# Tile numbers packed four to a word, and an alternating order of adds in the joint pass of a graph network kernel

## The reference

```
x = layernorm(x + gated(x))      # a_in  = segment_sum(f_in[src] * w,  dst); a_out = segment_sum(f_out[dst] * w2, src)
x = layernorm(x + relational(x)) # agg   = segment_sum((x @ W[type])[src], dst)
x = layernorm(x + attention(x))  # softmax over the edges of a node, segment_max and segment_sum
x = layernorm(x + relational(x)) # agg   = segment_sum((x @ W[type])[dst], src)
```

## Time and profile before

| | |
|---|---|
| time, median of 3 runs | 8551.53 us (8549.6 to 8559.96) |
| span of the profiled execution | 8619.9 us |
| busy: PE, DVE, ACT, POOL | 4852.2, 3573.0, 1730.7, 5243.4 us |
| granted TensorE clock, mean | 0.742 |

### The profile page before, as it was taken

How to read it: one execution, slowest core, us unless ns; L and a number is a source line. 1 busy time by engine, 2 the same in 40 slices (tenths; PEclk the granted TensorE clock), 3 DMA queues, 4 the chain that set the end, 5 groups by cost and what they waited for, 6 DMA issues and landing times. The chain is left out here.

```text
span 8619.9 us, 69117 instructions
## 1 busy us (share of the span) xinstructions
PE 4852.2 (56%) x17004; PEld 2990.1 (35%) x17004; DVE 3573.0 (41%) x9196; ACT 1730.7 (20%) x7055; POOL 5243.4 (61%) x5610
## 2 busy tenths in 40 slices
PE   3202235555557777777455543777777876655554
PEld 1100014444435555543333332222223663333332
DVE  4201014333335555564222224444445776244445
ACT  0000001111123333322000002222223874000000
POOL 5577756666666666632666662666665882366665
PEclk6655557777778888888666666878888998866666
DMA  3001012222235555554333335656666884333333
GB/s 96 2 3 39 15 40 90 90 89 89 91 116 176 177 175 175 177 114 156 92 93 93 92 93 67 186 184 187 187 187 177 267 271 156 117 93 92 91 94 85
DMA packets 422550, 1037.69 MB, mean 120 GB/s; under 512 B 159993, under 2 KB 188189, under 8 KB 415516
## 3 DMA queue, kind: packets, MB, share of 16 engines
q0 software_dynamic: 223616, 552.46, 22.9%
q1 hardware_dynamic: 198556, 480.95, 17.4%
HBM read 716.74 MB, written 316.30 MB: 120 GB/s over the span
## 5 line engine op out<-in xcount | busy, mean ns | idle before, releaser
L944 POOL DMA_INDIRECT rel_rows<-relation_rows,rel_ring_row x1640 | 1558.3, 950 | 1177.7 <-ACT rel_ring_end L937 695.1
L956 PE MATMUL rel_sums<-rel_rows,rel_hot 128*128 128x256 f32 x3280 | 1197.1, 509 | 1178.3 <-issue 448.5
L956 PEld LDWEIGHTS rel_sums<-rel_rows,rel_hot 128*128 128x128 f32 x3280 | 785.7, 252 | 1590.1 <-issue 1076.9
L982 DVE TENSOR_TENSOR g_acc<-rel_sums,g_acc 128x256 f32 x1224 | 517.8, 423 | 1532.9 <-DMA records_by_dst<-g_big 548.5
L1913 POOL DMA_INDIRECT nmax_rows<-messages,nmax_ring_row x832 | 788.6, 948 | 566.3 <-ACT nmax_ring_row L1869 327.6
L761 POOL DMA_INDIRECT rows_by_src<-spread_rows,spread_ring_place x832 | 803.2, 965 | 483.8 <-issue 254.3
L838 POOL DMA_INDIRECT both_rows<-batch_normed,both_ring_row x832 | 791.0, 951 | 460.9 <-ACT both_ring_end L807 231.3
L605 POOL DMA_INDIRECT records_by_dst<-sort_ring_rec,sort_ring_place x784 | 810.4, 1034 | 390.6 <-issue 241.2
L739 PE MATMUL spread_p_r<-g_big,spread_hot_t 128*128 x1664 | 631.5, 545 | 542.0 <-ACT spread_hot_t L674 358.8
L1961 DVE TENSOR_TENSOR g_big<-nmax_short,g_big 128x512 f32 x832 | 575.7, 692 | 659.9 <-PE nmax_short L1934 288.6
L1934 PE MATMUL nmax_short<-nmax_rows,g_ident_b 128*128 128x512 bf16 x2496 | 800.3, 436 | 0.0
(11 more groups left out here) (443 smaller groups left out, 6114.8 us busy)
## 6 DMA issues: line engine op xcount, KB each, us to landing
kept_rows<-nmax_rows SPq DMA_DIRECT2D x208, 536.0 KB
g_big<-kept_rows SPq DMA_DIRECT2D x208, 536.0 KB
both_out_rows<-rows_by_src SPq DMA_DIRECT2D x202, 520.0 KB
att_local_row<-local_of_edge SPq DMA_DIRECT2D x52, 512.0 KB
rel_rows<-relation_rows,rel_ring_row POOLq DMA_INDIRECT x1640
relation_rows<-mix_table SPq DMA_DIRECT2D x25, 1024.0 KB
relation_rows<-fin_table SPq DMA_DIRECT2D x25, 1024.0 KB, 3.9
rows_by_src<-spread_rows,spread_ring_place POOLq DMA_INDIRECT x832
```

Of the source, the lines that this page charges most:

```text
L944: pool.indirect_dma_start(rows[:, j, 0:words], None, table, bass.IndirectOffsetOnAxis(ap=ring_row[:, j:j + 1], axis=0)).then_inc(landed[n ...
L956: last = nc.tensor.matmul(sums[:, unit % slots, 0:width], hot[:, j, :], rows[:, j, :], start=of == 0, stop=of == GRAIN[k] - 1)
L982: nc.vector.tensor_tensor(at, sums[:, unit % slots, 0:width], at, ALU.add).then_inc(added, 1)
```

## The change

The tile numbers are packed. `sort_edges` keeps `unit_tile` as a tile of its own and, when the last places are worked out, folds four numbers, of 5 bits each, into one 32-bit word of `g.unit_word[k]`: three small instructions on DVE for each list, with a wait behind each. `tiles_of` loads 4 words in place of 16 numbers and returns 16 expressions (shift by 5n, mask with 31). At each place that uses a tile number, `compute_val` works out shift and mask into a register of that engine; for the adds this stands ahead of the wait for the add before.

In the joint pass the order of DVE changes. Before, one step was four out adds, four matrices, two in adds of the same group. Now step n is out add, in add, out add, in add, out add, two matrices, out add, two matrices, and its in adds belong to group n-1.

```diff
+            for k in range(2):
+                word, tile = g.unit_word[k][0:1, :], unit_tile[k][0:1, 0:PACK * WORDS[k]]
+                for n in reversed(range(PACK - 1)):
+                    c.step(nc.vector.scalar_tensor_tensor(word, tile[:, PACK - 1::PACK] if n == PACK - 2 else word,
+                                                          float(B32), tile[:, n::PACK], ALU.mult, ALU.add))
+                    c.wait()
...
             def target(k, acc, unit):
                 if unit % 16 == 0:
                     tiles[k][:] = tiles_of(nc, mybir.EngineType.DVE, g, k, unit)
-                return acc[:, bass.ds(tiles[k][unit % 16], 1), 0:width].rearrange("p t d -> p (t d)")
+                tile = nc.vector.compute_val(tiles[k][unit % 16])
+                return acc[:, bass.ds(tile, 1), 0:width].rearrange("p t d -> p (t d)")
...
-            build(0)
-            build(1)
-            for n in range(GROUPS):
-                if n < OUT_GROUPS:
-                    add_out(n)
+            def step(n):
+                outs = list(range(n * PER[1], (n + 1) * PER[1])) if n < OUT_GROUPS else []
+                ins = list(range((n - 1) * PER[0], n * PER[0])) if n else []
+                if outs:
+                    dve.wait_ge(out_summed, n + 1)
+                    add_out(outs[0])
+                if ins:
+                    dve.wait_ge(summed, n)
+                for at in range(PER[0]):
+                    if ins:
+                        add_in(ins[at])
+                    if outs:
+                        add_out(outs[at + 1])
                 if n + 2 < GROUPS:
-                    build(n + 2)
-                add_in(n)
+                    build(n + 2, 0, GRP // 2)
+                if outs:
+                    add_out(outs[-1])
+                if n + 2 < GROUPS:
+                    build(n + 2, GRP // 2, GRP)
...
 def tiles_of(nc, engine, g, k, unit):
 
-    return nc.values_load_multi_w_load_instructions(
-        g.unit_tile[k][0:1, unit:min(unit + 16, CHUNKS[k] // GRAIN[k])], engines=[engine], min_val=0, max_val=T,
-        skip_runtime_bounds_check_because="sort_edges counts them up from 0 and cuts them off at T")[1]
+    first = unit // PACK
+    words = nc.values_load_multi_w_load_instructions(
+        g.unit_word[k][0:1, first:min(first + 16 // PACK, WORDS[k])], engines=[engine], min_val=0,
+        max_val=T * sum(B32 ** n for n in range(PACK)),
+        skip_runtime_bounds_check_because="each packs PACK numbers that sort_edges cuts off at T")[1]
+    return [nc.s_assert_within((word >> (5 * n)) & (B32 - 1), 0, T,
+                               skip_runtime_bounds_check_because="sort_edges cuts every number off at T")
+            for word in words for n in range(PACK)]
```

More of the change, by code:

```diff
@@ L47 @@
 GROUPS = CH // GRP
+PACK = 4
+WORDS = tuple(chunks // grain // PACK for chunks, grain in zip(CHUNKS, GRAIN))
 CHP = -(-(P * EC + BUCKETS * (2 * P - 1)) // (2 * P)) * 2 + GRP
@@ L220, in sort_edges @@
         ones_last = m.sb("ones_last", [P, P])
+        unit_tile = [m.sb(f"unit_tile_{k}", [P, CHP // GRAIN[k]], I32) for k in range(2)]
         p_mean = m.ps("p_mean", [P, 2, 512])
@@ L866, in _, with build @@
             tiles = [[], []]
-            def build(n):
+            def build(n, lo, hi):
                 dve.wait_ge(staged, n + 1)
-                for j in range(slot(n).start, slot(n).stop):
+                for j in range(slot(n).start + lo, slot(n).start + hi):
                     last = nc.vector.tensor_scalar(hot[:, j, :], g.iota[:, 0:P], ring_end[:, j, 0:1],
                                                    ring_end[:, j, 1:2], ALU.is_equal, ALU.mult)
-                last.then_inc(hot_ready, 1)
+                if hi == GRP:
+                    last.then_inc(hot_ready, 1)
             def target(k, acc, unit):
@@ L877, in target @@
                     tiles[k][:] = tiles_of(nc, mybir.EngineType.DVE, g, k, unit)
-                return acc[:, bass.ds(tiles[k][unit % 16], 1), 0:width].rearrange("p t d -> p (t d)")
[L880 to L894, removed]
-            build(0)
-            build(1)
-            for n in range(GROUPS):
-                if n < OUT_GROUPS:
-                    add_out(n)
-                if n + 2 < GROUPS:
-                    build(n + 2)
-                add_in(n)
+                tile = nc.vector.compute_val(tiles[k][unit % 16])
@@ new lines, in target, with add_out, add_in @@
+                return acc[:, bass.ds(tile, 1), 0:width].rearrange("p t d -> p (t d)")
+            def add_out(unit):
+                at = target(1, g.acc2, unit)
+                if unit:
+                    dve.wait_ge(out_added, unit)
+                nc.vector.tensor_tensor(at, out_sums[:, unit % 4, 0:width], at, ALU.add).then_inc(out_added, 1)
+            def add_in(unit):
+                at = target(0, g.acc[:], unit)
+                if unit:
+                    dve.wait_ge(added, unit)
+                nc.vector.tensor_tensor(at, sums[:, unit % 4, 0:width], at, ALU.add).then_inc(added, 1)
@@ L904, in _ @@
+            for n in range(2):
+                build(n, 0, GRP)
+            for n in range(GROUPS + 1):
+                step(n)
             dve.wait_ge(added, GROUPS * PER[0])
@@ L1956, in _ @@
                     tiles = tiles_of(nc, mybir.EngineType.DVE, g, 0, unit)
+                if c % GRAIN[0] == 0:
+                    tile = nc.vector.compute_val(tiles[unit % 16])
                 dve.wait_ge(scored, c + 1)
@@ L2527, in build @@
         g.rec = [m.sb("rec_0", [P, CHP, RW]), m.sb("rec_1", [P, CHP, 2])]
-        g.unit_tile = [m.sb(f"unit_tile_{k}", [P, CHP // GRAIN[k]], I32) for k in range(2)]
+        g.unit_word = [m.sb(f"unit_word_{k}", [P, WORDS[k]], I32) for k in range(2)]
         make_constants(nc, g)
```

18 lines of the change are left out of this document (12 added, 6 removed).

## The result

The changed kernel takes 8571.14 us (median of 19 runs), the kernel before 8555.24 us beside it: ratio 1.0018, 95% interval [1.0012, 1.0024]. That is 16 us more, just inside the 0.2% that counts as no change here, and sure to be no gain. Forecast were 8496 us and a range of 8390 to 8570; the time lies outside it. One of the 19 runs took 8899 us at a granted clock of 0.59; the ratio goes by the others. A later set of runs gave 1.0018 [1.0009, 1.0027] again.

The account below looks back on a forecast made before the run. The prediction took POOL's indirect DMAs as the bound, with DVE counting only where POOL waits. Gains of 77 us (joint pass 50) less 22 us added gave -55 us: 8551.5 to 8496 us, range 8390 to 8570.

Parts of the forecast that it names:

- The bound: Joint pass: POOL's indirect DMAs and short gaps set a floor of 1049 us; about 203 us more is waiting for ACT.
- The sign that the prediction named: Joint pass: the forecast is wrong if POOL's waits (231.3 us, forecast about 180) stay as they are despite quicker steps.
- The loads: Register loads on DVE and PE: four words take 0.34 us, 0.76 us less than 16 numbers; 258 loads, mostly hidden.
- I take a third: Joint pass: of 155 us of pace from quicker DVE steps (order and loads), 50 us show as gain.
- At least one more such instruction: Unpacking: shift and mask add at least one register instruction ahead of each of 3280 adds and maxima and 832 PE uses.
- Behind a running add it costs nothing: Unpacking on DVE: the sequencer has 0.43 us for it during an add, ahead of the wait, so no cost shows.
- The +20 us of the sum: Unpacking's cost: +15 us at first adds of groups on DVE, +5 us on PE in spread.
- The price of the first add: First add of a group after DVE waited for PE: unpacking adds 0.12 us, counted for a fifth of groups, 15 us.
- Rival 1: Whole kernel: POOL hides the change's effect; about 8545 us, chance 0.17.
- Rival 2: Joint pass: the new order removes most of PE's 282.9 us of waits for out adds; about 8410 us, chance 0.17.
- rival 4: Register loads: a fixed cost makes four words take as long as 16; 8535 us, chance 0.06.
- Rival 3: Joint pass: alternating adds don't start 0.34 us apart, PE waits longer, its clock falls; 8580 to 8615 us, chance 0.13.

Follow-up runs that it names:

- e14: Kernel before with two register operations a unit more on DVE, in the aggregate passes alone: ratio 0.9992, in the set where the unchanged kernel took 7628 us.
- e5: The kernel before, unchanged, profiled a second time: span 8557.6 us.
- e13: Kernel before with tile numbers loaded 4 at a time for 4 units, old order, nothing packed: ratio 0.9975.
- e4: Kernel before with two register operations a unit more (shift and mask) in all passes, old order, 16 numbers a load: ratio 1.0127.
- e3: Kernel before with loads of 4 numbers, each used for four units (wrong tiles, less address work), no unpacking: ratio 0.9952.
- e6: Kernel before with the new order and loads of 4 numbers each used for four units (wrong tiles, less address work), no unpacking: ratio 0.9944.
- e1: Full change but with the joint pass's old order of adds and builds, against the kernel before: ratio 1.0038.
- e2: Kernel before with the new order of the joint pass alone, 16 plain numbers a load, no unpacking: ratio 0.9979.

## Why the prediction was wrong

**The bound: right.** POOL's gathers with their short gaps set the floor of about 1049 us for the joint pass, and the rest is POOL's waits for ACT. In the set of 7628 us the pass has 1061 us, and POOL waits (kernel e14, whose joint pass is that of before):

```profile
POOL both_rows L838 <- issue: 251.0, 824, 0.3
POOL both_rows L838 <- ACT both_ring_end L807: 2.7, 8, 0.6
...
2193.00:3254.00 1061.00, 777.41 (x3281) 613.19 (x3282) 721.22 (x2056) 463.29 (x1626) 788.83 (x832) 0.98 0.70 205
```

With DVE in its old order and busy just as long (721 us), the 200 us of waits are gone, and TensorE's granted clock is 0.98 in place of 0.86. What is gone with them are DVE's long standstills: between POOL's first and last gather of the pass DVE is idle for more than 5 us 33 times in the unchanged kernel (e5, 221 us together) and 42 times in the full change (348 us), but twice in e14 and e13. So DVE's work by itself doesn't keep POOL waiting. That it lengthens waits which these standstills begin fits e4, whose joint pass has 1290 us, but is argued and not shown. The sign that the prediction named came: POOL's waits stayed (212.5 and 217.2 us) in spite of quicker steps.

**The loads: right in size, wrong in place.** 0.34 us for four words, forecast and measured (0.343). The Trainium skill ("Runtime: NRT & Kernel Launch", "Instruction fetch mechanics") gives about 200 ns a register for a register load, which it describes as one from HBM; by it four words would be 0.8 us, an estimate. These loads are from SBUF, and the trace disagrees. The sum had 27 us for the other passes and about a quarter of the joint pass's 50, some 40 together; measured are 20 us (e13, four loads) to 41 (e3, with less address work). But attend, forecast at 3 us, gave 16 (e13) to 23 of them (e3): its 26 loads on each of two engines are 40 us at 0.76 us, and much of it showed.

**The order: the step that failed second.** The pace was right (0.34 us apart, DVE busy 67 us less in the pass). "I take a third" of 155 us was not: order and shorter loads together gave the joint pass 15 us (1250 to 1235 in e6), not 50. The order alone is worth 7 us (e3 to e6, 0.9952 to 0.9944), 17 us (e1 to the full change) or 18 us (e2) in the whole kernel. A faster recovery gave DVE time to wait in.

**The unpacking: the step that failed most.** "At least one more such instruction" was 1.75, not joined to the one for the address. "Behind a running add it costs nothing" holds between the adds of the joint pass and in rel3 outside the slow stretches, but the sum took it for everything that isn't the first add of a group or a gather in spread. The +20 us of the sum measured between some 53 and 74 us. The price of the first add was not the fault: where DVE has waited for PE, its register work takes 0.20 us in the full change against 0.12 before (medians in the joint pass, over the adds behind more than 0.8 us of idle time, those with a load left out), 0.09 more where 0.12 was taken. Left out was attend, where DVE, PE, ACT and POOL at 80% spoke against cover on every engine: two operations a unit cost 50 us there at their ordinary 0.045 us. Left out too were the slow stretches of rel3 (12 us in the full change). In the joint pass packing cost 15 us (e1); at which of its adds is not shown. Packing itself was put at 2 us, and no run shows it: the first scatter of spread starts at 1262.2 us in the full change and 1263.6 in e1, but also at 1262.4 in e3, which packs nothing.

Put together: packing with its loads and its unpacking is +33 us (e1), the order beside it -17 (e1 to the full change), and that is the +16. How the 33 divides between loads and unpacking is known only within the bounds above.

**The rivals.** Rival 1 (POOL hides it all, 0.17) had the joint pass right: its length hardly moved. (Its 8551 - 10 is 8541, not about 8545.) Rival 2 fell (PE's waits for out adds were not broken: 220.2 us in e5, 273.0 after), rival 4 too (0.343 us for four words). Rival 3 named a slower kernel, but by adds that would not alternate at 0.34 us; they do. The slowing came through the instruction count of all passes, which no rival had.

**Open.** What makes the stretches in which waits and register operations come in steps of about 0.7 us, and why one set of runs was 930 us shorter. The two go together: the set of 7628 us has neither the long standstills of the joint pass nor the slow stretches of rel3. Which is cause and which is effect, of these, the granted clock and the time, isn't shown. It isn't the chip by itself: the record gives the same chip number for the sets of 7628 and of 8601 us, and another one for both a set of 8555 and one of 8597. Slow fetching of every instruction doesn't fit, since the matrices inside keep their 0.2 us. It was not tried to provoke or remove the stretches.

## What to carry to other kernels

Cost the instructions that an engine's queue must issue, one by one, in the pass where several engines are all near 80% busy; a stall of 1.1 us per 16 units was worth less than 28 instructions of 0.045 us. Cut a long register load into short ones before you compress what it loads: loads of 4 plain numbers beat the unchanged kernel with either order of adds (0.9971, 0.9975), where packing lost. Count the register instructions of an experiment that leaves something out: here it left out the address work as well. And profile the reference twice before passes are compared: here its first profile lay 62 us above the second.

## What was not expected of the hardware

- The unchanged kernel took 8555 to 8601 us in most sets of runs and 7628 us in one (granted clock 0.82 in place of 0.74), and an edit that cost 0.18% in the one kind cost nothing in the other (0.9992 [0.9983, 1.0001]).
- In some stretches of 10 to 30 us register operations of 0.045 us are recorded with 0.7 or 1.4 us, on VectorE, and adds stand up to 4.2 us apart, while the building of its matrices runs on as ever. The set of 7628 us has none.
- Two operations a unit cost three times as much as one (109 and 36 us).
